# First attention of a two-layer transformer block: 512-column halves against 1024-column wholes, and a one-hot comparison in two halves

## The reference

```python
q = xt @ Wq.T                                    # xt: 16 x 256 x 128
scores = scale * jnp.einsum('bhqd,bhkd->bhqk', qh, qh)
logits = (scores * cmask + (1.0 - cmask) * NEG) * rmask
attn = jax.nn.softmax(logits, axis=-1)
ctx = jnp.einsum('bhqk,bhkd->bhqd', attn, qh)
out = ctx @ Wo.T
w = lut[idx]                                     # each of the three weight matrices after it
h = jax.nn.silu(gate) * up
```

## Time and profile before

| | |
|---|---|
| three runs, median (lowest to highest) | 627.96 us (624.17 to 632.28) |
| the profiled execution | 622.91 us, its span 621.2 us |
| PE busy | 539.9 us (87%) |
| DVE busy | 393.0 us (63%) |
| ACT busy | 329.1 us (53%) |
| POOL busy | 123.3 us (20%) |

### The profile page before, as it was taken

The page is one execution under the profiler, slowest core; times in us unless marked ns, Lnnn a source line. Parts: engine busy times, 40 slices in busy tenths (PEclk is TensorE's granted clock), DMA queues, the critical chain, the costliest instruction groups (busy, mean ns, idle before and its releaser), DMA issues. The chain is left out here.

```text
span 621.2 us, 14978 instructions
## 1 busy us (share of the span) xinstructions
PE 539.9 (87%) x4939; PEld 324.5 (52%) x4971; DVE 393.0 (63%) x812; ACT 329.1 (53%) x606; POOL 123.3 (20%) x164
## 2 busy tenths in 40 slices
PE   2799999999989999999699999973489999999962
PEld 1345555555554665655466656641246666555641
DVE  1677988989986555557699998886234433333330
ACT  2257777777775334445799999970122233223320
POOL 3302121212431200000000000000313333333310
PEclk9999999999999999999799999996599999999996
DMA  8865454555582452110955555551134445454440
GB/s 282 226 129 164 119 133 119 131 120 127 126 170 76 89 150 68 52 52 2 231 107 119 121 121 123 123 120 20 43 83 98 110 109 114 111 117 111 110 97 1
DMA packets 71879, 70.27 MB, mean 113 GB/s; under 512 B 46149, under 2 KB 60903, under 8 KB 69160
## 3 DMA queue, kind: packets, MB, share of 16 engines
q1 hardware_dynamic: 60752, 35.65, 22.7%
q0 software_dynamic: 8768, 18.46, 14.7%
q10 hardware_dynamic: 2328, 15.75, 10.3%
HBM read 58.75 MB, written 7.81 MB: 107 GB/s over the span
## 5 line engine op out<-in xcount | busy, mean ns | idle before, releaser
L1329 DVE TENSOR_REDUCE nmax<-PB 128x2 f32<-128x512 f32 x128 | 85.6, 682 | 20.7 <-PE PB L879 19.0
L564 ACT ACTIVATE probs<-PC 128x512 f32<-128x512 f32 x128 | 74.0, 610 | 20.3 <-PE PC L891 19.4
L1785 DVE TENSOR_TENSOR probs<-PB,probs 128x1024 f32<-128x1024 f32 x19 | 23.3, 1225 | 82.2 <-PE PB L1241 78.1
L879 PE MATMUL PB<-small 64*128 64x256 bf16 x256 | 51.1, 291 | 6.7 <-DVE nmax L1329 6.6
L1241 PE MATMUL PA<-arena,probs 128*128 x210 | 50.8, 392 | 6.6 <-DVE probs L1778 3.2
L1241 PE MATMUL PB<-arena,probs 128*128 x228 | 52.3, 379 | 0.0
L803 ACT ACTIVATE probs<-PA 128x1024 f32<-128x1024 f32 x19 | 19.5, 1025 | 59.1 <-PE PA L1241 41.9
L479 POOL DMA_DIRECT2D arena<-in_w_all x16 | 11.5, 716 | 192.0 <-DVE arena L1606 106.2
L891 PE MATMUL PC<-small 64*128 64x256 bf16 x256 | 45.6, 281 | 0.5 <-DVE small L1345 0.5
L501 POOL DMA_INDIRECT out<-probs,tokn x19 | 19.4, 1021 | 101.7 <-DVE probs L1798 101.7
L1241 PEld LDWEIGHTS PA<-arena,probs 128*128 128x128 bf16 x228 | 22.7, 100 | 30.6 <-issue 9.6
(11 more groups left out here) (214 smaller groups left out, 1132.5 us busy)
## 6 DMA issues: line engine op xcount, KB each, us to landing
arena<-idx_low ACTq DMA_DIRECT2D x15, 1024.0 KB
wst<-in_w_all SPq DMA_DIRECT2D x48, 256.0 KB, 2.8
arena<-in_w_all POOLq DMA_DIRECT2D x16, 256.0 KB, 5.2
arena<-in_idx_all SPq DMA_DIRECT2D x1, 2176.0 KB, 10.3
arena<-in_cond SPq DMA_DIRECT2D x16, 128.0 KB, 7.2
small<-in_x SPq DMA_DIRECT2D x16, 128.0 KB, 9.8
arena<-idx_low POOLq DMA_DIRECT2D x2, 1024.0 KB, 14.6
arena<-in_w_all POOLq DMA_DIRECT2D x2, 1024.0 KB, 10.3
```

Of the source, the lines that this page charges most:

```text
L564: nc.scalar.activation(probs[:, c, o], PC[:, o], ACT.Exp, scale=SCALE0).then_inc(S["ex"], 1)
L879: ins = mm(PB[:, s * 512 + qt * T:s * 512 + (qt + 1) * T], qs[r, par, c * T + qt * P:c * T + (qt + 1) * P], ks[r, par, c * T:(c + 1) * T], ...
L1329: v.tensor_reduce(nmax[:, c, s, :], PB[:, s * 512:(s + 1) * 512].rearrange("p (a k) -> p a k", k=T), AX.X, ALU.max, negate=True).then_inc( ...
L1785: v.tensor_tensor(hh, PB[:], gs, ALU.mult).then_inc(S["hm"], 1)
```

## The change

Maxima: `maximum(b, c)` is one reduce over both banks of PB (1024 columns, four results), and there are four a body. Exponentials: `exps(b, c)` is one activation over both banks of PC, also four a body. `scores(b, par, c)` fills both banks of PB for one pair c with four matmuls, in turn from the lower and the upper 64 rows, and waits for maximum c-1 (count 4b+c). `scores_T` does the same in PC and waits for exponential c-1. The counts of `sa`, `st`, `max` and `ex` are halved everywhere, and those of `onehot` doubled.

One-hot: the comparison is two instructions of 2048 columns, the first between maximum 1 and maximum 2 and the second between maximum 2 and `max_columns`; `look_up` runs as 16 and 16 matmuls, where it had 8, 8 and 16. Element 0's comparison, in body 1, moves the same way.

Order: on DVE, step 0 of `normalise` (the transpose) moves from the start of body i+1 to the end of body i, ahead of `add_max`; steps 1 and 2 and `low` now stand between maximum 0 and 1, step 3 behind maximum 1. On PE `place(i+1, 0)` and `outputs0(i-2)` stand ahead of `scores(2)`, `contexts(0)` behind scores_T(2), `contexts(1)` right behind scores_T(3). On ACT `context_out` and `looked_up` stand between exponentials 2 and 3. Not shown: the halved counts elsewhere, the prologue and the four exponential pairs behind the last body.

```diff
@@ -557,11 +557,10 @@
                 nc.scalar.copy(vu[:, par, :, :, 0:DK0], PD[:, 0:T].rearrange("p (k h d) -> p k h d", k=KT, h=H0)
                                ).then_inc(S["vu"], 1)
 
-            def exps(b, c, s):
+            def exps(b, c):
                 unless_first(act, S["ctx"], b)
-                act.wait_ge(S["st"], 8 * b + 2 * c + (1 - s) + 1)
-                o = slice(s * 512, (s + 1) * 512)
-                nc.scalar.activation(probs[:, c, o], PC[:, o], ACT.Exp, scale=SCALE0).then_inc(S["ex"], 1)
+                act.wait_ge(S["st"], 4 * b + c + 1)
+                nc.scalar.activation(probs[:, c, :], PC[:], ACT.Exp, scale=SCALE0).then_inc(S["ex"], 1)
 
             def context_out(b):
                 act.wait_ge(S["wo"], b + 1)
...
@@ -589,23 +588,18 @@
                     load_hot(i + 1, 1 - par)
                 if after:
                     high(i + 1)
-                exps(i - 1, 0, 1)
-                exps(i - 1, 0, 0)
+                exps(i - 1, 0)
                 values(i - 1, 1 - par)
-                exps(i - 1, 1, 1)
-                exps(i - 1, 1, 0)
+                exps(i - 1, 1)
                 if first:
                     looked_up(0)
                 if after:
                     stacks(i + 1, 1 - par, 0)
-                exps(i - 1, 2, 1)
+                exps(i - 1, 2)
                 if before:
                     context_out(i - 2)
-                exps(i - 1, 2, 0)
-                exps(i - 1, 3, 1)
-                if before:
                     looked_up(i - 1)
-                exps(i - 1, 3, 0)
+                exps(i - 1, 3)
                 if after:
                     stacks(i + 1, 1 - par, 1)
 
...
@@ -871,33 +864,35 @@
                     ins = mm(PD[:, kt * P:(kt + 1) * P], xs[:, par, kt * P:(kt + 1) * P], wq1[:], start=True, stop=True)
                 ins.then_inc(S["v"], 1)
 
-            def scores(b, par, c, s):
+            def scores(b, par, c):
                 pe.wait_ge(S["k3"], 4 * b + 2 * (c // 2) + 2)
-                unless_first(pe, S["max"], 8 * b + 2 * c + s - 1)
-                r = slice(64 * s, 64 * s + 64)
+                unless_first(pe, S["max"], 4 * b + c)
                 for qt in range(KT):
-                    ins = mm(PB[:, s * 512 + qt * T:s * 512 + (qt + 1) * T],
-                             qs[r, par, c * T + qt * P:c * T + (qt + 1) * P], ks[r, par, c * T:(c + 1) * T],
-                             start=True, stop=True)
+                    for s in range(2):
+                        r = slice(64 * s, 64 * s + 64)
+                        ins = mm(PB[:, s * 512 + qt * T:s * 512 + (qt + 1) * T],
+                                 qs[r, par, c * T + qt * P:c * T + (qt + 1) * P], ks[r, par, c * T:(c + 1) * T],
+                                 start=True, stop=True)
                 ins.then_inc(S["sa"], 1)
 
-            def scores_T(b, par, c, s):
+            def scores_T(b, par, c):
                 pp, kt = c // KT, c % KT
                 pe.wait_ge(S["q2"], b + 1)
-                unless_first(pe, S["ex"], 8 * b + 2 * c + (1 - s) - 1)
-                r = slice(64 * s, 64 * s + 64)
+                unless_first(pe, S["ex"], 4 * b + c)
                 for n in range(2):
                     pr = 2 * pp + n
-                    ins = mm(PC[:, s * 512 + n * T:s * 512 + (n + 1) * T],
-                             ks[r, par, pr * T + kt * P:pr * T + (kt + 1) * P], qs[r, par, pr * T:(pr + 1) * T],
-                             start=True, stop=True)
+                    for s in range(2):
+                        r = slice(64 * s, 64 * s + 64)
+                        ins = mm(PC[:, s * 512 + n * T:s * 512 + (n + 1) * T],
+                                 ks[r, par, pr * T + kt * P:pr * T + (kt + 1) * P], qs[r, par, pr * T:(pr + 1) * T],
+                                 start=True, stop=True)
                 ins.then_inc(S["st"], 1)
 
             def contexts(b, par, pp):
 
                 pe.wait_ge(S["vu"], b + 1)
                 unless_first(pe, S["c"], b)
-                pe.wait_ge(S["ex"], 8 * b + 4 * pp + 4)
+                pe.wait_ge(S["ex"], 4 * b + 2 * pp + 2)
                 for kt in range(KT):
                     for h in range(GROUP):
                         s, n = h % 2, h // 2
...
@@ -953,35 +949,30 @@
             def body(i, par, half, before=True, after=True, first=False):
                 other = 1 - par
 
-                def pair(c, s):
-                    scores(i, par, c, s)
-                    scores_T(i - 1, other, c, 1 - s)
-
-                scores(i, par, 0, 0)
+                scores(i, par, 0)
                 if after:
                     project(i + 1, other)
-                scores_T(i - 1, other, 0, 1)
-                pair(0, 1)
+                scores_T(i - 1, other, 0)
                 project_v(i - 1, other, half)
-                pair(1, 0)
+                scores(i, par, 1)
                 if before:
-                    look_up(i - 1, other, range(0, 1)) if not first else look_up(0, 0, range(0, 2))
-                pair(1, 1)
-                if before:
-                    look_up(i - 1, other, range(1, 2)) if not first else look_up(0, 0, range(2, 4))
+                    look_up(i - 1, other, range(0, 2)) if not first else look_up(0, 0, range(0, 4))
+                scores_T(i - 1, other, 1)
                 if after:
                     place(i + 1, other, 0)
-                pair(2, 0)
                 if before:
                     outputs0(i - 2)
-                pair(2, 1)
-                if before:
-                    look_up(i - 1, other, range(0 if first else 2, 4))
-                pair(3, 0)
+                scores(i, par, 2)
+                if before and not first:
+                    look_up(i - 1, other, range(2, 4))
+                scores_T(i - 1, other, 2)
+                if first:
+                    look_up(1, other)
                 contexts(i - 1, other, 0)
-                pair(3, 1)
+                scores(i, par, 3)
                 if after:
                     place(i + 1, other, 1)
+                scores_T(i - 1, other, 3)
                 contexts(i - 1, other, 1)
                 max_rows(i)
 
...
@@ -1309,24 +1299,28 @@
                                     ).then_inc(S["lutw"], 1)
 
 
-            def one_hot(c, par, half):
-                if isinstance(c, int) and c < 2:
-                    dve.wait_ge(S[f"hot_first{c}"], 16)
-                else:
-                    dve.wait_ge(S[f"hot{par}"], 16 * half)
-                unless_first(dve, S["lmm"], c - 1)
-                v.tensor_scalar(hot[:, par, :], spread[:, par, :], cst[:, C_V:C_V + 1], None, ALU.is_equal).then_inc(S["onehot"], 1)
+            def one_hot(c, par, half, parts=range(2)):
+                if 0 in parts:
+                    if isinstance(c, int) and c < 2:
+                        dve.wait_ge(S[f"hot_first{c}"], 16)
+                    else:
+                        dve.wait_ge(S[f"hot{par}"], 16 * half)
+                    unless_first(dve, S["lmm"], c - 1)
+                for n in parts:
+                    o = slice(n * LHOT // 2, (n + 1) * LHOT // 2)
+                    v.tensor_scalar(hot[:, par, o], spread[:, par, o], cst[:, C_V:C_V + 1], None, ALU.is_equal
+                                    ).then_inc(S["onehot"], 1)
 
             def low(b):
                 dve.wait_ge(S["ph"], b + 1)
                 unless_first(dve, S["pq"], 2 * b)
                 v.tensor_tensor(pl[:], PA[:, 0:T], ph[:], ALU.subtract).then_inc(S["pl"], 1)
 
-            def maximum(b, c, s):
-                dve.wait_ge(S["sa"], 8 * b + 2 * c + s + 1)
-                if c == s == 0:
+            def maximum(b, c):
+                dve.wait_ge(S["sa"], 4 * b + c + 1)
+                if c == 0:
                     unless_first(dve, S["mc"], 3 * b)
-                v.tensor_reduce(nmax[:, c, s, :], PB[:, s * 512:(s + 1) * 512].rearrange("p (a k) -> p a k", k=T),
+                v.tensor_reduce(nmax[:, c].rearrange("p s q -> p (s q)"), PB[:].rearrange("p (a k) -> p a k", k=T),
                                 AX.X, ALU.max, negate=True).then_inc(S["max"], 1)
 
             def max_columns(b):
...
@@ -1334,8 +1328,8 @@
                 unless_first(dve, S["mt"], b)
                 v.tensor_copy(mcol[:, :, :, ROW_ABSENT::64].rearrange("p q r s -> p q (r s)"),
                               nbig[:, :, bass.ds(b, 1)].broadcast_to([P, KT, 2 * PAIRS])).then_inc(S["mc"], 1)
-                maximum(b, 3, 1)
-                dve.wait_ge(S["max"], 8 * b + 8)
+                maximum(b, 3)
+                dve.wait_ge(S["max"], 4 * b + 4)
                 v.tensor_copy(cols[:, :, :, :, ROW_MAX], nmax[:]).then_inc(S["mc"], 1)
                 dve.wait_ge(S["mc"], 3 * b + 2)
                 v.tensor_tensor(cols[:, :, :, :, ROW_MAX_LOW], nmax[:], cols[:, :, :, :, ROW_MAX], ALU.subtract).then_inc(S["mc"], 1)
...
@@ -1364,33 +1358,29 @@
```

(43 more changed lines are left out.)

8 lines of the change are left out of this document (4 added, 4 removed).

## The result

The changed kernel takes 695.5 us (median of 4, 687.8 to 698.39), the kernel before, run beside it, 630.12 us: ratio 1.1013, 95% interval 1.0867 to 1.1159. The profiled execution took 698.08 us, span 696.4, against 622.91: 75.2 us more.

A forecast was written before the change was run, and what follows sets the result against it. The prediction took DVE for the bound, 9.4 of a 10.48 us body. A start 4.1 us late and bodies of 12.8 us made 33 us: 656 us profiled, 661 on the runs' scale, range 641 to 684.

The forecast's parts named there:

- steps 1 to 6: Steady loop body, followed from one DVE add through DVE, PE and ACT to the next: 12.8 us instead of 10.48.
- Half of it: Rival, loop body: contexts(0) not held by the copy, 1.48 us goes, body 11.3 us, time 643 us; chance 0.09.
- the list of signs: Closing list of what a trace would show if right, such as adds 12.8 us apart, or if wrong.
- Later loads: One-hot row loads after element 2's: they have a whole longer body to land and cost nothing.
- The clock: Rival, loop: TensorE falls to 1.2 GHz, some 4.5 us more a body; half of bodies 690, all 720; chance 0.09.
- a mild clock loss: Upper edge of the forecast range, 684 us, meant to cover a small loss of TensorE's clock.
- The start: Body 2: DVE waits 5 us for element 2's load, so its add comes at 58.1 instead of 54.00, 4.1 late.
- as equal: Prologue and body 1 taken to last as long as before: wider waits, fewer starts, PE's slow matmuls there.
- the same landing: Element 2's one-hot rows assumed to arrive at 51.99 as before, with DVE waiting 5 us for them.
- The sum: Whole kernel: last add at 223.5 against 190.20, 33 us later; profiled 656 us, 661 on the scale of the runs.
- the two halves are no longer independent: Loop: scores(c) waits for maximum c-1 and scores_T(c) for exponential c-1, each wait holding all behind it on PE.
- the 0.5 by which DVE's work was to fall: DVE, loop body: four maxima of 1024 columns instead of eight of 512 save 0.5 us a body.

The follow-up runs named there:

- e2: Changed kernel with ACT's context_out moved ahead of exponential 2: 651.37 us, ratio 1.0407 to the kernel before.
- e3: e2 with DVE's normalise step 3 also moved ahead of maximum 1: 641.22 us, ratio 1.0258 to the kernel before.
- e1: Changed kernel with matmuls that nothing reads added in PE's pauses, 10 ahead of contexts(0) and 6 ahead of contexts(1): 668.98 us, ratio 1.0691.
- e10: e1 with the one-hot comparisons of bodies 1 and 2 put back behind the maxima: 664.07 us, ratio 1.0641.
- e7: Kernel before with only the one-hot comparison split into two halves between the maxima, in every body: 637.74 us, ratio 1.0125.
- e4: Kernel before with only DVE's order changed, maximum (0,1) straight behind (0,0) and the normalise steps later: 619.02 us, ratio 0.9884.
- e8: e4 with PE's look-ups moved forward, the first 8 ahead of the projection of v: 615.75 us, ratio 0.9751.
- e5: Changed kernel's order, with scores, turned scores, maxima and exponentials in halves of 512 columns, each with its own wait: 701.5 us, ratio 1.1093.
- e9: e5 with three repairs: copy ahead of exponentials 2, normalise step 3 ahead of maximum 1, comparisons of bodies 1 and 2 late: 634.56 us, ratio 1.0169.

## Why the prediction was right or wrong

**The chain, steps 1 to 6: right to 0.12 us.** Counted from the add at 170.53: maximum 1 lets the next instruction in at 3.79 (forecast 3.78); the outputs start at 4.28 and scores_T(2) at 5.74 (4.26, 5.72); contexts(0) start at 7.56 (7.53); exponential 3 at 9.97 (9.96); contexts(1) at 11.14 (11.04); the next add at 12.91 (12.79). DVE's waits of 0.50, 1.64 and 1.55 were given as 0.5, 1.7 and 1.4. e2 and e3 show that the holders are those named: without the copy's hold a body takes 11.36, where *Half of it* had 11.3. PE's two waits are 1.43 and 1.21; the steps give 1.41 and 1.13, though the list of signs has "about 1.1 each". Later loads cost nothing, as said: behind 62 us no wait of DVE for a load is in the trace.

**The clock: the step that failed.** It was left as a rival at 0.09, on the ground that the full clock held in the earlier trace rows and that each body has long dense pieces. But the earlier trace rows show it for a PE whose records cover 108.72 of 114 us, and here they cover 9.61 of 12.90, which leaves the three idle us that the rival itself had counted. So the step that failed is a term that the sum put at nothing: PE's pieces were priced at the full clock in all 13 bodies, and the range allowed only "a mild clock loss". The runs showed the lower clock in nearly all of them, worth 32 us in the profile and 26.5 between the medians (e1). In the body sampled at 149 the clock fell right behind the pause of 1.43. The rival's 4.5 us a body were too much: the slow bodies are 2.8 to 3.1 us longer than 12.91, since the clock is back up for a part of each. Its half of the bodies at 690 and all at 720 enclose the 695.5, but that 690 comes so near is luck: twelve of the 13 bodies were longer than 12.91, each by less than was put down. e1 shows that idle time of PE is the cause, and e2 that without the pause of 1.43 the clock stayed up. Why the body that ends at 183.44 was spared, and the one at 170.53 in part, with the same pauses, stays open.

**The start: half seen.** The forecast found the wait of element 2's comparison and took the prologue and body 1 "as equal". But the change moves body 1's comparison in the same way, to before its load is there. DVE waited 5.24 there, body 1 took 20.5 us for 14.8, and PE stood still. Nor was it "the same landing" for element 2: its load was issued 3.7 us later and was there about 3 us later, and DVE waited 2.17 for it instead of 5. Together 7.7 us instead of 4.1; e10 returns 4.9 of them.

**The sum.** With the clock held the changed kernel takes 668.98 us, with the start repaired as well 664.07. The forecast of 661 was the price of the chain, and the chain's own range, 652 to 671, holds both. The clock's 26.5 us took the result out of it. In the profiled executions, 656 forecast and 698.1 measured, 41.3 of the 42 us are the clock's 32.2, the start's 3.6, 13 x 0.12 = 1.6 of the chain, the 3.7 behind the last add, and the gain of 0.2 that was forecast there.

**What bounds the kernel before: wrong, without harm to the sum.** The prediction took DVE for the bound, at 9.4 of 10.48 us. e7 fills DVE's gaps and gains nothing in the loop, and e4 reorders the same work and gains 0.54 a body: a chain that crosses the engines, not DVE's sum of work, set the period. Which waits make it up was not followed link by link; that e8 gains another 0.13 by moving PE's look-ups alone says that PE's queue is in it. The prediction also began the chain with "the two halves are no longer independent"; e5 and e9 show that in this order independent halves are no faster. The loss lies in where the copy, step 3 and the contexts stand.

**The gain of wider instructions.** Wholes against halves in the repaired order are worth 10.98 - 10.85 = 0.13 us a body, not the 0.5 by which DVE's work was to fall. (DVE's busy time fell by 3.4 us in all, about half of what that makes in 13 bodies.) The Trainium skill, Perfetto Trace Analysis, section "Optimizing Scalar/DVE Operations", says that grouping can improve throughput if the engine is saturated; DVE wasn't, and the small gain agrees. Its other advice, which the prediction set against the change, to break instructions up where they cause bubbles on other engines, gained nothing in this order (e5, e9): there the bubbles came from where the instructions stood.

**Not shown singly:** what the remaining 0.37 us of a repaired body (10.85 against 10.48) is. PE still waits 1.21 us for exponential 3 before contexts(1), and the transpose now stands between those and the add; no run moved them.

## What to carry to other kernels

Before merging instructions or buffers, write one period as a chain through every engine's queue, and ask of each instruction what stands behind it while it waits: the busiest engine need not be the bound, and a gap that is filled there may only move. If that chain gives TensorE more idle time in a period than any stretch of the trace has at the full clock, the lower clock belongs into the forecast itself and not among remote rivals; it is no certainty either, for in e2 the full clock held with PE busy 105.25 of 125 us. And a wait for a load is to be looked for in every body that is written out, the first one too, along with the later loads whose issue it delays.

## What the runs showed of the hardware that was not expected

TensorE fell to its lower level, 1.2 GHz, over and over in a loop whose longest pause at full clock was 1.43 us: granted clock 0.76 over 60 to 235 us, contexts of 1.94 us for 1.07. Without that one pause (e2) it was 1.00 over 75 to 200 us, and with matmuls whose results nothing reads in the pauses (e1) 0.94, with the kernel 26.5 us faster.

The granted clock doesn't show all: in e4 it was 1.00 over 41 to 57 us, where the contexts took 1.93 us, and in the kernel before 1.00 over 35 to 37 us, where those of the earlier trace rows took 1.93. Near the start the length of a known matmul is the surer sign.
